# Reordering the opening routing of a two-layer expert kernel

## The reference, cut to what matters

```python
x = x + 0.5 * ffn(layernorm(x), gate_w, wi_gate, wi_up, wo)
x = x + attn(layernorm(x), ...)
x = x + 0.5 * ffn(layernorm(x), gate_w, wi_gate, wi_up, wo)

# ffn: 8 experts, each token's best 2, capacity 640
p = softmax(x @ gate_w.T);  top_p, top_i = top_k(p, 2);  top_p /= top_p.sum(-1)
for k in range(2):
    hot = (top_i[:, k, None] == arange(8))
    pos = cumsum(hot, axis=0) - 1            # place in the expert's queue, by token order
    keep = pos_of_own_expert < 640           # later tokens are dropped
    rows = scatter tokens into (expert, pos);  y = (silu(rows @ wi_gate.T) * (rows @ wi_up.T)) @ wo.T
    out += where(keep, top_p[:, k] * y[expert, pos], 0)
```

## Time and profile before

| what | value |
|---|---|
| median of 3 runs | 917.46 us (914.82, 917.46, 926.24) |
| the profiled execution | 921.84 us, its span 920.0 us |
| PE busy in the span | 845.3 us (92%) |
| DVE, ACT, POOL busy | 547.2, 392.8, 500.8 us |
| mean granted TensorE clock | 0.953 |

### The profile page before, as it was taken

One profiled execution on the slowest core, in us unless ns is written; L12 is line 12 of the kernel. 1 busy time (PEld: TensorE's weight loads), 2 busy tenths in 40 slices (PEclk: granted clock), 3 DMA queues, 4 the chain that ended last, 5 costly groups with the idle time before them and its releaser, 6 DMA issues. The chain is left out here.

```text
span 920.0 us, 26251 instructions
## 1 busy us (share of the span) xinstructions
PE 845.3 (92%) x10885; PEld 747.1 (81%) x10885; DVE 547.2 (59%) x1645; ACT 392.8 (43%) x850; POOL 500.8 (54%) x631
## 2 busy tenths in 40 slices
PE   8479999999979789999999899998989999999996
PEld 7358999999967566788778776877767899999996
DVE  4745665555557945658485936484573556656662
ACT  4634444444314432266346542562542544444431
POOL 2658889866630721582228623882445444346667
PEclk8569999999989899899999999999998999999998
DMA  9454677444222110012001121111112644445544
GB/s 310 111 117 122 214 232 251 133 137 135 61 85 58 24 33 18 4 24 54 20 5 30 38 75 39 22 35 52 51 47 78 223 154 153 128 128 115 118 67 36
DMA packets 75475, 85.97 MB, mean 93 GB/s; under 512 B 9767, under 2 KB 62163, under 8 KB 74332
## 3 DMA queue, kind: packets, MB, share of 16 engines
q1 hardware_dynamic: 61148, 63.74, 23.3%
q0 software_dynamic: 14208, 20.55, 9.7%
HBM read 46.70 MB, written 34.01 MB: 88 GB/s over the span
## 5 line engine op out<-in xcount | busy, mean ns | idle before, releaser
L1020 DVE TENSOR_TENSOR e_hid<-e_sg,e_pu 128x320 f32<-128x320 f32 x256 | 124.7, 488 | 160.5 <-ACT e_sg L961 153.9
L961 ACT ACTIVATE e_sg<-e_pg 128x320 f32<-128x320 f32 x256 | 111.9, 438 | 208.5 <-PE e_pg L918 208.1
L282 POOL DMA_INDIRECT queue<-wide_rows,slot x64 | 64.9, 1014 | 89.5 <-ACT wide_rows L568 21.1
L1112 POOL TENSOR_TENSOR first_rows<-a_inv,a_nmat 128x135 f32<-128x135 f32 (+20 forms) x116 | 61.2, 527 | 68.7 <-DVE a_nmat L1965 60.2
L916 PE MATMUL e_pg<-e_xlo,e_whi 128*128 128x320 f32 x256 | 96.6, 377 | 0.9 <-DVE e_xlo L983 0.5
L904 PE MATMUL e_po<-e_expert,e_hid 128*128 128x128 f32 x640 | 83.7, 275 | 1.3 <-DVE e_hid L1020 1.3
L904 PE MATMUL e_po<-expert,e_hid 128*128 128x128 f32 x640 | 84.2, 274 | 0.0
L904 PEld LDWEIGHTS e_po<-e_expert,e_hid 128*128 128x128 f32 x640 | 79.9, 191 | 1.8 <-DVE e_hid L1020 1.8
L904 PEld LDWEIGHTS e_po<-expert,e_hid 128*128 128x128 f32 x640 | 80.3, 191 | 0.1
L917 PE MATMUL e_pg<-e_xhi,e_wlo 128*128 128x320 f32 x256 | 79.7, 311 | 0.0
L918 PE MATMUL e_pu<-e_xhi,e_whi 128*128 128x320 f32 x256 | 79.5, 310 | 0.0
(11 more groups left out here) (379 smaller groups left out, 2076.8 us busy)
## 6 DMA issues: line engine op xcount, KB each, us to landing
expert<-wexp_in SPq DMA_DIRECT2D x14, 512.0 KB, 4.4
e_expert<-wexp_in SPq DMA_DIRECT2D x14, 512.0 KB, 4.4
line<-blank SPq DMA_DIRECT2D x3, 1310.0 KB, 7.4
e_xs<-queue SPq DMA_DIRECT2D x12, 327.5 KB, 4.9
e_xs<-line SPq DMA_DIRECT2D x6, 647.5 KB, 6.4
expert<-wexp_in SPq DMA_DIRECT2D x14, 256.0 KB, 2.8
e_expert<-wexp_in SPq DMA_DIRECT2D x14, 256.0 KB, 3.5
queue<-blank SPq DMA_DIRECT2D x2, 1310.0 KB, 9.3
```

What stands on the lines that cost most here:

```text
L282: pool.indirect_dma_start(io.queue, bass.IndirectOffsetOnAxis(ap=k.slot[:, j, 1:2], axis=0), k.xn[:, j, :], None, bounds_check=SLOTS - 1, ...
L961: act.activation(sg[n % 2][:], pg[n % 2][:, 0:HALF], ACT.Silu).then_inc(silued, 1)
L1020: dve.tensor_tensor(hid[q % 2][:, f, c * HALF:c * HALF + HALF], sg[n % 2][:], pu[n % 2][:, 0:HALF], ALU.mult).then_inc(hidden, 1)
L1112: link(eng.tensor_tensor(part, bc(inv[:, j:j + 1, own], shape), bc(factor, shape), ALU.mult))
```

## The change

Five things change, all in `route`:

- `tally`, `seen` and the running count go. Each group keeps its own one-hot tile `hot[g]`, and PE counts the groups before by itself: `count_past(g)` issues one all-ones matmul of 128 columns for each of the 8 g earlier tiles. Places alternate between two PSUM tiles.
- `level` is taken out of `rank` into `level_out(g)`, which stands earlier in DVE's list (ahead of `assign` or `mark` of the group before).
- Group 0's x is loaded in halves, the constants first; `turn` and `score` go by halves, and so do group 0's statistics. Group 3's table write is in halves too.
- PE's order: group 1 to 3 are turned and scored as one piece; `list_spots` of a group follows `count` or `count_past` of a later one.
- ACT's order: `normalise(0)` ahead of `keep(2)`, `normalise(1)` ahead of `squares(2)`. DVE's order: `mark` ahead of `factor`, `one_hot(3)` ahead of `factor(3)`, the two `gap` steps last.

```diff
 SP
+            def keep_rows(g, begin=0, end=GRP):
+                if end < GRP:
+                    sp.wait_ge(halved, 1)
+                else:
+                    sp.wait_ge(normed, g + 1)
+                sp.dma_start(table_rows(io.table, g)[:, begin:end, :],
+                             k.xn[:, g * GRP + begin:g * GRP + end, :]).then_inc(k.tabled, 16)
-            sp.dma_start(k.x[:, own(0), :], x[:, own(0), :]).then_inc(xgot[0], 16)
             sp.dma_start(k.const[:], io.const).then_inc(cgot, 16)
+            sp.dma_start(k.x[:, 0:HALF_GRP, :], x[:, 0:HALF_GRP, :]).then_inc(opened, 16)
             sp.dma_start(k.gate[:, 0:E], io.gate).then_inc(cgot, 16)
             sp.dma_start(tri[:], io.tri).then_inc(cgot, 16)
+            sp.dma_start(k.x[:, HALF_GRP:GRP, :], x[:, HALF_GRP:GRP, :]).then_inc(xgot[0], 16)
...
-            keep_rows(3)
+            keep_rows(3, 0, HALF_GRP)
+            keep_rows(3, HALF_GRP, GRP)
 DVE
+            def level_out(g):
+                dve.wait_ge(scored, g + 1)
+                dve.tensor_scalar(level[:, own(g)], scores(g)[:, :, E], -1.0 / D, None, ALU.mult).then_inc(levelled, 1)
-            def tally(g):
-                link(dve.tensor_reduce(more[:], hot[:].rearrange("p a b c -> p (b c) a"), AX.X, ALU.add))
-                link(dve.tensor_tensor(k.count[:], k.count[:], more[:], ALU.add))
-                dve.tensor_copy(seen[(g + 1) % 2][:, 0, :], k.count[:])
...
             one_hot(0)
-            tally(0)
+            level_out(1)
             rank(1)
             assign(0)
             one_hot(1)
-            tally(1)
+            mark(0)
             factor(1)
-            mark(0)
+            level_out(2)
             assign(1)
             rank(2)
             one_hot(2)
-            tally(2)
+            level_out(3)
+            mark(1)
             factor(2)
-            mark(1)
             assign(2)
             rank(3)
+            one_hot(3)
             factor(3)
-            one_hot(3)
             mark(2)
+            assign(3)
+            mark(3)
 ACT
             keep(1)
+            normalise(0)
             keep(2)
-            normalise(0)
             squares(1)
             root(1)
             keep(3)
+            normalise(1)
             squares(2)
             root(2)
-            normalise(1)
             squares(3)
 PE
+            def count_past(g):
+                pe.wait_ge(counted, g)
+                behind(pe, slotted, g - 1)
+                for j in range(g * GRP):
+                    flat = hot[j // GRP][:].rearrange("p a b c -> p a (b c)")
+                    pe.matmul(ppos[g % 2][:, 0:GRP * TOPK * E], k.ones[:],
+                              bc(flat[:, j % GRP:j % GRP + 1, :], [P, GRP, TOPK * E]), start=(j == 0), stop=False)
...
+            for n in range(2):
+                turn(0, n)
+                score(0, n)
+            turn_and_score(1)
             count(0)
+            turn_and_score(2)
+            count_past(1)
             count(1)
+            turn_and_score(3)
+            count_past(2)
+            list_spots(0)
+            keep_clock(pe, k, pidle, 8)
+            count(2)
+            count_past(3)
+            list_spots(1)
+            keep_clock(pe, k, pidle, 8)
+            count(3)
             keep_clock(pe, k, pidle, 6)
             list_spots(2)
             keep_clock(pe, k, pidle, 10)
             list_spots(3)
 POOL
-            pool.wait_ge(k.tabled, 16 * (NGRP + 1))
+            pool.wait_ge(k.tabled, 16 * (NGRP + 2))
```

More of the change, by code:

```diff
@@ L360, in route @@
         top, index = sb("top", [P, NT, 8]), [sb(f"index{i}", [P, GRP, 8], U32) for i in range(2)]
-        hot = sb("hot", [P, GRP, TOPK, E], BF16)
-        seen = [sb(f"seen{i}", [P, 1, TOPK * E], BF16) for i in range(2)]
-        more = sb("more", [P, TOPK * E])
+        hot = [sb(f"hot{i}", [P, GRP, TOPK, E], BF16) for i in range(NGRP)]
         prod, pos = sb("prod", [P, GRP * TOPK, E]), sb("pos", [P, GRP, TOPK])
@@ L426, in _, with first_statistics @@
             link = steps.done
-            def first_statistics():
-                dve.wait_ge(xgot[0], 16)
-                for j in range(GRP):
+            def first_statistics(half):
+                dve.wait_ge(xgot[0] if half else opened, 16)
+                for j in range(half * HALF_GRP, half * HALF_GRP + HALF_GRP):
                     last = dve.bn_stats(stat[:, j, :], k.x[:, j, :])
                 link(last)
+                if not half:
+                    return
                 for j in range(GRP):
@@ L569, in normalise @@
                                           scale=rstd[:, j:j + 1])
+                    if j == NT - 1 - HALF_GRP:
+                        last.then_inc(halved, 1)
                 last.then_inc(normed, 1)
@@ L598, in _, with turn @@
         def _(pe):
[L599 to L608, removed]
+            def turn(g, n):
+                if g or n:
+                    pe.wait_ge(xgot[g], 16)
+                else:
+                    pe.wait_ge(opened, 16)
+                behind(pe, evac, 2 * g + n - 1 if g else 0)
+                for j in range(HALF_GRP):
+                    mm = pe.transpose(ptr[:, n, j * P:j * P + P], k.x[:, g * GRP + n * HALF_GRP + j, :],
+                                      k.const[:, C_ID:C_ID + P])
+                mm.then_inc(turned, 1)
@@ new lines, in turn_and_score @@
+            def turn_and_score(g):
+                turn(g, 0)
+                turn(g, 1)
+                keep_clock(pe, k, pidle, 4)
+                score(g, 0)
+                score(g, 1)
+            def count_past(g):
[5 more added lines that the diff above has]
+                              bc(flat[:, j % GRP:j % GRP + 1, :], [P, GRP, TOPK * E]), start=(j == 0), stop=False)
@@ L625, in count @@
[L625 to L626 removed]
+                    mm = pe.matmul(ppos[g % 2][:, (j + 1) * TOPK * E:GRP * TOPK * E], k.ones[:],
+                                   bc(flat[:, j:j + 1, :], [P, GRP - 1 - j, TOPK * E]), start=False,
+                                   stop=(j == GRP - 2))
+                mm.then_inc(placed, 1)
             def list_spots(g):
@@ L641, in _ @@
             keep_clock(pe, k, pidle, 4)
-            for g in range(2):
-                turn(g)
-                keep_clock(pe, k, pidle, 4)
-                score(g)
-            turn(2)
+            for n in range(2):
+                turn(0, n)
+                score(0, n)
+            turn_and_score(1)
             count(0)
-            score(2)
-            keep_clock(pe, k, pidle, 4)
+            turn_and_score(2)
+            count_past(1)
             count(1)
-            turn(3)
-            keep_clock(pe, k, pidle, 6)
-            list_spots(0)
-            score(3)
-            keep_clock(pe, k, pidle, 6)
-            list_spots(1)
-            count(2)
-            keep_clock(pe, k, pidle, 12)
+            turn_and_score(3)
[7 more added lines that the diff above has]
+            count(3)
+            keep_clock(pe, k, pidle, 6)
             list_spots(2)
-            count(3)
             keep_clock(pe, k, pidle, 10)
```

53 lines of the change are left out of this document (22 added, 31 removed).

## The result

The changed kernel takes 913.88 us (median of 20 runs, 909.01 to 920.81) where the kernel before takes 920.53 in 20 runs of its own (914.82 to 926.24, the three runs of the prediction among them). The ratio is 0.9934, 95% interval 0.9916 to 0.9952: 6.1 us faster, 4.4 to 7.7 on the scale of 917.46, and, as forecast, within two per cent. The forecast was 7.6.

A forecast was written before the change was run, and what follows sets the result against it. The prediction took the experts as bound by PE and the opening's end as set by ACT's list through the last table write. -6.97 + 0.6 = -6.4, then -1.2, gave -7.6: 917.46 to 909.9 us, range 904 to 919.

The forecast's parts named there:

- What ends the opening: End of the opening: the last table write releases the first gather, the gate matmul follows 7.14 us behind.
- Levels ahead, -6.97: ACT ahead of `squares(2)` and `squares(3)`: both waits on `level` go, -6.97 us; levels out at 23.1 and 26.9.
- Group 0 in halves, +0.6: PE's `score(0)`: two waits of about 0.8 us replace one of 0.39, +0.6 us; wrong if not later than 11.6.
- the rival of the low clock: "The clock stays low": PE's clock falls at 12 to 14 us and stays low; gain 2 to 4 us; chance 0.16.
- Halved write, -1.2: Group 3's table write: half issued 1.5 us sooner, -1.2 us; wrong if the last half lands 8 us behind issue.
- The sum: Opening and whole time: -6.4 and -1.2 give -7.6 us, gather at 48.1, time 909.9 us; chance 0.62.
- Counts by PE, nothing: PE and DVE: about 0.85 us leaves DVE four times, off the path; `count_past(1)` takes 0.9 us on PE.
- Marks ahead of roots, nothing: DVE's list: `factor(1)` behind `mark(0)` ends at 23.0, wanted at 24.9; a spots table 1.9 us late costs nothing.
- The whole rest moves: Behind the opening: nothing hangs on its own clock, so what the opening gains or loses moves the whole rest.
- Writes at their bare time: Rival on the table's writes: the gather starts when `inverse` is written, 44.4; gain 11.2 us, 906.3 us; chance 0.12.
- Slower: Rival on PE in group 0: clock falls at 9 us and stays low; +0.8 us, 918.3 us; chance 0.05.
- It does not matter: Rival behind the opening: a slot or landing not seen takes the gain back, 917.5 us; chance 0.05.

The follow-up runs named there:

- f: The changed kernel with `level` put back inside `rank`, all other lists as changed: 914.27 us, ratio 0.9935 to the kernel before.
- a: The kernel before with only the levels taken out of `rank` as steps of their own: 914.46 us, ratio 0.9955 to the kernel before.
- h: The changed kernel with group 0 whole again (one load of x ahead of the constants, statistics in one piece): 910.31 us, ratio 0.9889.
- c: The changed kernel with seven `keep_clock` matmuls ahead of each half `score` of group 0: 906.51 us, ratio 0.9874.
- b: The changed kernel with group 3's table write in one piece again: 913.70 us, ratio 0.9937.
- d: The changed kernel with table rows of 512 bytes in place of 524, the last three columns left out: 909.88 us, ratio 0.9891.
- g: The changed kernel with the running count (`tally`) back on DVE and no `count_past`: 911.18 us, ratio 0.9903.
- n: The changed kernel with each of PE's `list_spots` ahead of the next counts, as in the old order: 914.56 us, ratio 0.9958.
- k: j with 15 scatters ahead of the first gather in place of 18, three sent later: 915.77 us, ratio 0.9967 to the kernel before.
- e: The changed kernel with the edits of c and d together: 905.40 us, ratio 0.9845.
- j: The changed kernel with group 0 whole, the running count on DVE, `factor(1)` ahead of `mark(0)` and table rows of 512 bytes: 909.21 us, ratio 0.9898.

## Why the prediction held, point by point

**What ends the opening.** Right. The table releases the gather before and after, the gate matmul follows 7.05 us behind (forecast 7.14), and `inverse` and POOL are not binding: 45.74 and 46.61 against 50.83. POOL's scatters were 20.9 us in all, not 18.9, which is 2.0 of the 3.0 us by which its forecast of 43.6 was early.

**Levels ahead, -6.97.** Right. The levels were out at 23.0 and 27.7 (forecast 23.1 and 26.9) and both waits are gone. *f* shows that the other parts do as much without them, and *a* that the levels alone bring 4.1.

**Group 0 in halves, +0.6.** The mechanism and the two waits of 0.8 us were right: counted from PE's start, `score(0)` ended 5.4 us on, where the kernel before took 4.5. But by the prediction's own sign (`score(0)` not later than 11.6) the step failed, as PE did not start at 7.15 in both orders. And the term left out the clock. It fell at 11.5 us, a little ahead of the rival of the low clock (12 to 14), and *h* and *c* put the whole cost at some 4 to 5.5 us. It was hidden in the sum for two reasons. The walk had already taken the low clock for `score(2)`, and PE started 1.66 us sooner, where 0.5 was the bound. Part of that is the order of the loads and part is scatter: PE's first real matmul starts at 5.5 to 6.1 us in the eight traces with the halved load and at 6.1 to 7.6 in the six with the whole one. `score(0)` ended at 10.87 in place of 12.2, and `turn(3)` released ACT at 24.75 in place of 23.8, so 2.3 us went between them that the walk did not have: `score(1)` at the low clock (3.42, not 1.92) and `turn(2)` (1.95, not 1.07 as in *c*).

**Halved write, -1.2.** Wrong; this is the step that failed, and the prediction's own sign for it came: the last half still released the gather 8.73 us behind its issue. Forecast was a landing 10.0 us behind group 2's issue, measured 11.80. *b* and the landings beside it show no gain. *d* shows what slows the tail, rows of 524 bytes in a write close behind another (140 to 171 GB/s); with rows of 512 the table is off the path. That engines busy already with group 2's rows gain nothing from an earlier half fits this, but no run shows it apart.

**The sum.** The gather was to start at 48.1 and started at 50.83. Of the 2.7 us, 0.9 is group 2's issue (39.03, not 38.1) and 1.8 the landing. Without the -1.2 the same sum reads 6.4, within 0.3 of the measured 6.1, but that nearness is partly luck: the earlier start and the low clock offset each other in it, and the opening of the traced execution gained 4.9, not 6.1. The time itself was forecast at 909.9 and is 913.88; 3.1 of these 4.0 us are the median of the kernel before, which is 920.53 in 20 runs and was 917.46 in three. As a time, 913.88 even lies in the band of the rival of the low clock (913.5 to 915.5); as a gain, 6.1 lies between that rival's 2 to 4 and the forecast's 6.4 to 9.1, and its interval reaches into the forecast's band alone.

**Counts by PE, nothing.** The wait of ACT for `turn(3)` was foreseen (2.4, measured 2.36). *g* puts 0.8 us of it on `count_past(1)`, against 0.9 in the walk. Its eight matmuls took 1.01 us at a granted clock of 0.50 and the sixteen of `count_past(2)` 1.05 at 1.00 (after). *n* shows that, with the levels out, counts ahead of lists matter for `inverse`.

**Marks ahead of roots, nothing.** Right while PE is slow: `normalise(1)` doesn't wait in after. In *h* it waits 1.94 us, so the cover was the low clock: 0.50 from 11.5 to 25.1 us in after, 1.00 until 26.3 in *h*.

**The whole rest moves.** On average only. The profiled span fell by 9.6 us, of which the opening has 4.9; the rest has 4.0, where the code is the same. Over all traces but *k*'s the rest was 645.9 to 656.4 long, with stretches at the low clock in different places (340 to 400 us read 0.86 to 0.97 in the kernel before, and 0.99 or more in *c*, *e* and *j*). Why *j*, with the opening of *e*, is 3.8 us slower is not settled.

**The rivals.** *Writes at their bare time* did not happen; in *d*, with rows of 512 bytes, the table is off the path and `inverse` is next. The 320 KB write that spoke for it is from the first layer, not from the opening, and its rows have 512 bytes. *The clock stays low*: it fell a little before that rival said and came back at 25 us, and the start was earlier, so the gain was 6.1 and not 2 to 4. *Slower* needed `score(3)` to end past 35 us; it ended at 27.5. *It does not matter* is excluded by the interval.

## What to carry to other kernels

When a small product stands in one engine's list behind work that needs another engine, move either: two cures of the same wait brought it once here (4.1 and 6.0 us apart, 6.1 together). Splitting the first step of a pipeline to start earlier can cost more than it gains: here the halves left TensorE waiting 0.78 us twice, and group 0 whole was some 4 us better (*h*). Fill such waits (14 idle matmuls brought 5.5 us here, *c*) before judging the split. Before cutting a transfer in pieces, look at the rate at which its bytes move: here a write of rows of 524 bytes close behind another was slow (140 to 171 GB/s), and rows of 512 bytes cured that (227 to 292) where halves did not.

## What the runs showed of the hardware that was not expected

- Two writes of 524-byte rows in a row: 282 to 285 GB/s for the first two microseconds, then 140 to 171; with 512-byte rows 213 to 292 throughout (after, *d*). A write of 524-byte rows that stood alone moved 209 and 277 (*a*).
- The last bytes and the release are apart: in *c* the windows show less than 100 GB/s from 43 us on, and the gather was still held by the table until 47.83. What it waits for is not shown.
- The granted clock fell at different times with the same list of PE: just ahead of 17 us in the kernel before, at 12.6 in *a*, whose PE program is unchanged. With group 0 in halves and unfilled waits it fell between 10.4 and 11.5 in all of six traces, and came back between 13.9 and 35.2; with filled waits or group 0 whole in the new lists, it fell between 18.1 and 26.3 in five of six (7.5 in *k*, where PE had waited 2.23 us for the triangle).
- An indirect DMA with 1.0 us of POOL's time took 1.4 to 2.0 in four of after's 18 scatters.
